# A graph-network kernel: gate stage in interleaved groups of four tiles, edge scatters moved into the node stages

## What is computed

```python
x = layernorm(x + x @ M)                  # M: product of 50,000 plane rotations, from src, dst, edge_weight
gate = sigmoid(relu(concat(x, query) @ gate_w1 + gate_b1) @ gate_w2 + gate_b2)
x0 = x * gate
h = concat(x0, query, x * query)
h = relu(rgat(h, W1, q1, k1, b1))         # relational attention: per edge score of query[dst] + key[src],
h = h + relu(rgat(h, W2, q2, k2, b2))     # softmax over the edges of a dst, weighted sum of rows of src;
h = relu(rgat(h, W3, q3, k3, b3))         # 4, 4 and 1 heads, two edge types with their own weights
x = layernorm(x + normalize(h @ proj_w + proj_b + x0))
x = layernorm(x + filtered_convolution(x, edge_attr))   # messages of src, summed by dst
x = layernorm(x + mean_of_neighbours(x))                # messages of dst, summed by src
```

## Time and profile before

| | before |
|---|---|
| three timed executions, us | 7099.04, 7114.69 (median), 7123.21 |
| the profiled execution, us | 7115.9 |
| its span in the trace, us | 7113.4 |
| TensorE busy (share of the span) | 4547.6 us (64%) |
| VectorE busy | 3329.0 us (47%) |
| ScalarE busy | 1981.2 us (28%) |
| GpSimd busy | 3666.5 us (52%) |
| granted TensorE clock, mean of the span | 0.753 of full speed |

### The profile page before, as it was taken

How to read it: one execution, slowest core, us unless ns; L and a number is a source line. 1 busy time by engine, 2 the same in 40 slices (tenths; PEclk the granted TensorE clock), 3 DMA queues, 4 the chain that set the end, 5 groups by cost and what they waited for, 6 DMA issues and landing times. The chain is left out here.

```text
span 7113.4 us, 82941 instructions
## 1 busy us (share of the span) xinstructions
PE 4547.6 (64%) x18412; PEld 3288.7 (46%) x18413; DVE 3329.0 (47%) x7794; ACT 1981.2 (28%) x4571; POOL 3666.5 (52%) x2933
## 2 busy tenths in 40 slices
PE   5699466642176677747666824448777777775553
PEld 5588444431155554435555723334455555443332
DVE  5577311126555452255554323343577777623334
ACT  0122111110055451035443112221455555510000
POOL 0344200001477664577664478870577777318885
PEclk9999767765588788978777655555799999876655
DMA  0000111111365542356553312221222222213333
GB/s 6 24 10 10 48 39 39 38 49 33 74 170 154 138 133 71 69 140 162 145 145 89 47 37 45 46 44 65 58 58 59 58 59 59 58 60 95 84 84 74
DMA packets 502900, 511.80 MB, mean 72 GB/s; under 512 B 324196, under 2 KB 387673, under 8 KB 502387
## 3 DMA queue, kind: packets, MB, share of 16 engines
q0 software_dynamic: 359872, 381.65, 22.4%
q1 hardware_dynamic: 142768, 127.70, 6.5%
HBM read 440.99 MB, written 65.22 MB: 71 GB/s over the span
## 5 line engine op out<-in xcount | busy, mean ns | idle before, releaser
L1198 POOL DMA_INDIRECT sum_gx_sb<-scratch_xw,keep_k_row_step_sb x1296 | 1617.8, 1248 | 575.2 <-issue 361.0
L1291 PE MATMUL sum_a_ps<-sum_gx_sb,sum_sel_sb 125*125 125x258 f32 (+1 forms) x4320 | 1227.9, 449 | 584.8 <-ACT sum_gx_sb L1233 229.9
L1291 PEld LDWEIGHTS sum_a_ps<-sum_gx_sb,sum_sel_sb 125*125 125x125 f32 x4320 | 947.3, 245 | 783.7 <-issue 592.6
L1233 ACT ACTIVATE sum_gx_sb<-sum_gx_sb,sum_wt_sb 125x129 f32<-125x129 f32 x3024 | 897.3, 388 | 446.5 <-DVE sum_wt_sb L1422 446.5
L2188 POOL DMA_INDIRECT filter_gx_sb<-scratch_h,keep_k_src_step_sb x432 | 523.6, 1212 | 310.7 <-DVEq L2332 164.7
L2619 POOL DMA_INDIRECT source_gx_sb<-scratch_h,source_grouped_sb x432 | 533.9, 1236 | 156.4 <-issue 122.9
L1109 POOL DMA_INDIRECT scratch_grouped<-keep_k_value_sb,keep_k_place_sb x400 | 542.2, 1356 | 132.3 <-issue 132.3
L2631 PE MATMUL source_s_ps<-source_gx_sb,source_sel_sb 125*125 125x257 f32 x864 | 375.8, 610 | 312.2 <-DMA source_gx_sb<-scratch_h,source_grouped_sb 310.6
L2237 PE MATMUL filter_ps<-filter_m_sb,filter_h_sb 128*125 128x256 f32 x1760 | 439.3, 406 | 38.6 <-DVE filter_f_sb L2301 37.4
L2631 PEld LDWEIGHTS source_s_ps<-source_gx_sb,source_sel_sb 125*125 125x125 f32 x864 | 249.8, 302 | 438.1 <-issue 173.5
L762 POOL DMA_INDIRECT order_near_i_sb<-in_dst,order_tile_i_sb x25 | 33.0, 1319 | 812.2 <-DVEq L796 804.9
(11 more groups left out here) (494 smaller groups left out, 7863.8 us busy)
## 6 DMA issues: line engine op xcount, KB each, us to landing
sum_gx_sb<-scratch_xw,keep_k_row_step_sb POOLq DMA_INDIRECT x1296, 4.3
scratch_xw<-gate_xsb_sb SPq DMA_DIRECT2D x50, 253.9 KB
scratch_xw<-attend_xsb_sb SPq DMA_DIRECT2D x50, 253.9 KB
filter_ea_sb<-in_ea_t SPq DMA_DIRECT2D x444, 24.4 KB
filter_gx_sb<-scratch_h,keep_k_src_step_sb POOLq DMA_INDIRECT x432
source_gx_sb<-scratch_h,source_grouped_sb POOLq DMA_INDIRECT x432, 4.0
sum_mk_sb<-scratch_masks SPq DMA_DIRECT2D x72, 93.9 KB
scratch_grouped<-keep_k_value_sb,keep_k_place_sb POOLq DMA_INDIRECT x400
```

What stands on the lines that cost most here:

```text
L1198: nc.gpsimd.indirect_dma_start(out=gx[:, q, j, :], out_offset=None, in_=table, in_offset=bass.IndirectOffsetOnAxis(ap=keep["row_step"][:, ...
L1233: last = nc.scalar.activation(here, here, ACT.Copy, scale=wt[q][:, h, j:j + 1])
L1291: last = mm(psa[b][0:P, half, 0:BF], sel[:, p, j, :], gx[:, q, at, half * BF:(half + 1) * BF], **flags)
```

## The change

1. The edge lists are made before the gate stage; `mt` is kept until then.
2. The gate stage is rewritten without a loop, in seven groups (six of four tiles, one of one tile). For each group the turn is made in halves of two tiles, two groups ahead; transposes, the two gate products, Relu, Sigmoid and the multiplication each work on up to 500 columns at once. The four steps of the next group's gate stand between the tables of this group's four tiles. The square root and the reciprocal become one power on GpSimd. The copy of the transposed x1 moves to ScalarE. The small products of the table are four of 16 columns in place of eight of 8. Table rows have two sets of PSUM banks and three SBUF buffers, each with its own store semaphore.
3. GpSimd issues in the gate stage six `group_edges` DMAs and one query scatter for each tile; in the first `nodes_attend` six and one (before: five), in the second four and one (before: three), in `filter_sum` none. `attention` loses its 25 scatters and the load of `qn`.
4. The queries stay in SBUF for all tiles (`qsb`) and are stored once, at the end of a node stage.

```diff
+def put_queries(nc, qe, keep, t, qsb, sem):
+    nc.gpsimd.indirect_dma_start(
+        out=qe, out_offset=bass.IndirectOffsetOnAxis(ap=keep["q_row"][:, t:t + 1], axis=0),
+        in_=qsb[:, t].rearrange("p r h -> p (r h)"), in_offset=None).then_inc(sem, 16)
 def attention(nc, mem, dr, keep, agg, heads, width, layer):
...
         def _(pool):
-            pool.wait_ge(nodes_in, 16)
-            for t in range(NT):
-                nc.gpsimd.indirect_dma_start(
-                    out=qe, out_offset=bass.IndirectOffsetOnAxis(ap=keep["q_row"][:, t:t + 1], axis=0),
-                    in_=qn[:, t], in_offset=None).then_inc(put, 16)
             for c in range(NEC):
...
-            sp.dma_start(qn[:], q_table.rearrange("(t p) s -> p t s", p=P)).then_inc(nodes_in, 16)
...
-            sp.wait_ge(put, 16 * NT)
             edges = qe[0:E, :].rearrange("(c p l) s -> c p (l s)", p=EC, l=P)
...
+GROUPS = [range(a, min(a + 4, NT)) for a in range(0, NT, 4)]
+def nodes_gate(nc, mem, dr, keep, mt):
+    LAST, GN, RING = len(GROUPS) - 1, 4, 3
...
+        def _(sp):
+            load_turned(0)
+            load_turned(1)
+            sp.dma_start(xn[:], dr["x"].rearrange("(t p) c -> p t c", p=P)).then_inc(xn_in, 16)
...
+            def store_rows(t):
+                sp.wait_ge(taken, t + 1)
+                for r in range(2):
+                    sp.dma_start(rows(dr["xw"], t, r * N), xsb[:, t % RING, r, :]).then_inc(xw_out[t % RING], 16)
...
+            for g in range(LAST + 1):
+                if g + 2 <= LAST:
+                    sp.wait_ge(y_taken, halves_of[g][-1] + 1)
+                    load_turned(g + 2)
+                sp.wait_ge(x1_made, g + 1)
+                sp.dma_start(by_node("x1", g), xn[:, tiles(g)]).then_inc(x1_out, 16)
+                sp.wait_ge(x0_made, g + 1)
+                sp.dma_start(by_node("x0", g), x0[:, 0:len(GROUPS[g])]).then_inc(x0_out, 16)
+                if g:
+                    for t in GROUPS[g - 1]:
+                        store_rows(t)
...
+        def _(pool):
+            def root(g):
+                pool.wait_ge(var_made, g + 1)
+                nc.gpsimd.tensor_tensor(rsd[:, tiles(g)], var[:, tiles(g)], power[:, 0:len(GROUPS[g])], ALU.pow).then_inc(
+                    rsd_made, 1)
+            root(0)
+            root(1)
+            for g in range(LAST + 1):
+                for j, t in enumerate(GROUPS[g]):
+                    if j == min(2, len(GROUPS[g]) - 1) and g + 2 <= LAST:
+                        root(g + 2)
+                    group_edges(nc, pool, dr, keep, range(6 * t, 6 * t + 6), grouped)
+                    pool.wait_ge(taken, t + 1)
+                    put_queries(nc, dr["qe"], keep, t, qsb, put)
...
+        def _(pe):
+            def table(t):
+                if t:
+                    pe.wait_ge(taken, t)
...
+            for g in range(LAST + 1):
+                ahead = halves_of[g + 2] if g + 2 <= LAST else []
+                own, nxt = GROUPS[g], g + 1 <= LAST
+                links = [lambda: turn_x1(g + 1), lambda: gate_hidden(g + 1), lambda: gate_outer(g + 1), lambda: turn_x0(g + 1)]
+                for j in range(GN):
+                    if j == 0 and ahead:
+                        turn(ahead[0])
+                    if nxt:
+                        links[j]()
+                    if j == 1 and len(ahead) > 1:
+                        turn(ahead[1])
+                    if j < len(own):
+                        table(own[j])
...
+        def _(dve):
+            def take(t):
+                dve.wait_ge(projected, t + 1)
+                if t >= RING:
+                    dve.wait_ge(xw_out[t % RING], 32 * (t // RING))
...
+                for j, t in enumerate(own):
+                    take(t)
+                    if j == 0 and len(ahead) > 1:
+                        residual(ahead[1])
+                    if j == min(1, len(own) - 1) and ahead:
+                        statistics(g + 2)
+                    if j == min(2, len(own) - 1):
+                        if g + 1 <= LAST:
+                            gate(g + 1)
+                        if ahead:
+                            scale(g + 2)
 def nodes_attend(nc, mem, dr, keep, agg, bias, names, width, heads, first):
...
                     pool.wait_ge(h_made, t + 1)
                     pool.dma_start(rows(dr["h1"], t), hc[:]).then_inc(kept_out, 16)
-                    group_edges(nc, pool, dr, keep, range(5 * t, 5 * t + 5), grouped)
+                    group_edges(nc, pool, dr, keep, range(6 * NT + 6 * t, 6 * NT + 6 * t + 6), grouped)
+                    if t:
+                        pool.wait_ge(table_made, 2 * t + 1)
+                        put_queries(nc, dr["qe"], keep, t - 1, qsb, put)
...
-                    group_edges(nc, pool, dr, keep, range(5 * NT + 3 * t, 5 * NT + 3 * t + 3), grouped)
+                    group_edges(nc, pool, dr, keep, range(12 * NT + 4 * t, 12 * NT + 4 * t + 4), grouped)
+                    if t:
+                        pool.wait_ge(table_made, 2 * t + 1)
+                        put_queries(nc, dr["qe1"], keep, t - 1, qsb, put)
...
 def filter_sum(nc, mem, dr, keep, agg):
...
-                if j == HF - 1 and step < 400:
-                    group_edges(nc, pool, dr, keep, range(8 * NT + step // 2 - 1, 8 * NT + step // 2 + 1), grouped)
-            pool.wait_ge(grouped, 16 * 200)
```

More of the change, by code:

```diff
@@ L1659, in _, with turn @@
         @block.tensor
         def _(pe):
+            def turn(k):
+                g, some = HALVES[k]
+                pe.wait_ge(xt_in[g % 2], 16 * (g // 2 + 1))
+                if k:
+                    pe.wait_ge(y_taken, k)
+                for j, t in enumerate(some):
+                    at = (t - GROUPS[g].start) * P
+                    for b in range(2):
+                        last = mm(psy[0:P, j, :], xt[:, g % 2, b, at:at + P], mt[:, b, :], start=(b == 0), stop=(b == 1))
+                last.then_inc(y_made, 1)
@@ L1661, in _ @@
+            turned = 0
+            for k in halves_of[0]:
+                turn(k)
             pe.wait_ge(landed, 16 * LOADS)
@@ L1741, in _, with residual, statistics @@
+            for g in range(LAST + 1):
+                take_x1(g)
+                hidden(g)
+                gate(g)
+                take_x0(g)
         @block.vector
         def _(dve):
+            def residual(k):
+                g, some = HALVES[k]
+                dve.wait_ge(y_made, k + 1)
+                here = slice(some.start, some.stop)
+                vec.tensor_tensor(xn[:, here], psy[0:P, 0:len(some), :], xn[:, here], ALU.add).then_inc(y_taken, 1)
+            def statistics(g):
+                dve.drain()
+                for t in GROUPS[g]:
+                    vec.bn_stats(stats[:, t, :], xn[:, t, :])
+                dve.drain()
+                for t in GROUPS[g]:
+                    vec.bn_aggr(mv[:, t, :], stats[:, t, :])
+                dve.drain()
+                vec.tensor_scalar(var[:, tiles(g)], mv[:, tiles(g), 1], 1e-5, None, ALU.add).then_inc(var_made, 1)
@@ L1799, in _ @@
-            residual(0)
-            with dve.Fori(0, NT - 1) as t:
-                gate(t)
-                residual(t + 1)
-                take(t)
-            gate(NT - 1)
-            take(NT - 1)
+            for k in halves_of[1]:
+                residual(k)
+            statistics(1)
+            gate(0)
+            scale(1)
+            for g in range(LAST + 1):
+                ahead = halves_of[g + 2] if g + 2 <= LAST else []
+                own = GROUPS[g]
+                if ahead:
+                    residual(ahead[0])
+                for j, t in enumerate(own):
[7 more added lines that the diff above has]
+                            gate(g + 1)
+                        if ahead:
+                            scale(g + 2)
@@ L2730, in build @@
             source_order(nc, mem, dr, keep)
+        with phase("gate") as mem:
+            nodes_gate(nc, mem, dr, keep, mt)
         agg = keeper.sb("agg", [P, NT + 1, 516])
```

298 lines of the change are left out of this document (166 added, 132 removed).

## The result

The changed kernel takes 6789.5 us (median of four runs, 6778.4 to 6793.9), the kernel before 7110.3 beside it. The ratio is 0.9548, with a 95% interval of 0.9530 to 0.9566. The forecast was 6762 with a range of 6708 to 6850: the sign and the range held, the time forecast was 27.5 us too low. The profiled execution spans 6788.7 us against 7113.4, so 324.7 us went where the sum had 353.

A forecast was written before the change was run, and what follows sets the result against it. No engine was full: the gate stage was a chain in which TensorE idles. Gate -284, edge stages -117, attends +30 and +18 sum to -353 us from 7115.9, forecast 6762 us, range 6708 to 6850.

The forecast's parts named there:

- Gate stage, TensorE's work: Gate stage: tables, turn, gate products and transposes give TensorE 43.7 us of work for four tiles.
- The wait for `turn_x0`: Gate stage, ahead of each group's fourth table: TensorE has nothing for some 3 us while VectorE finishes the third take.
- The ring: Gate stage: the fourth tile's take needs the first row's store, behind a 500 KB store; 1 us allowed.
- The tail: End of the gate stage: 6 us until the stores have landed and the next stage begins.
- GpSimd in the gate: Gate stage: GpSimd needs 44.4 us a group beside TensorE's 48.5, with 4 us of room.
- The rival that DMAs are delayed by VectorE: Gate stage and attends: delayed DMAs average 1.66 us, GpSimd becomes the bound, +47 us, 6809 in total; chance 0.20.
- Edge stages: Three edge stages: query loads or gathers start earlier, -37, -37 and -43 us, sum -117.
- Attends: Both attends: GpSimd's added DMAs set the pace, +30 us in the first and +18 in the second.
- Filter: Filter: VectorE's own instructions cover the scatters, so removing 200 DMAs gives 0 us.
- The clock rival: Gate and attends: TensorE's clock stays low, gate +75 us, attends +10, total 6845; chance 0.17, shared with exposed links.

The follow-up runs named there:

- rows_first: Changed kernel with SyncE storing a group's first three tables before it waits for x0 of the next group: 6752.1 us, gate stage 411.6.
- ring4: Changed kernel with four table buffers instead of three, order of stores unchanged: 6770.6 us, gate stage 410.8.
- no_gate_edges: Changed kernel with the gate stage's 150 edge scatters put into the filter instead: gate stage 428.2 us.
- the undo: Changed kernel with the query scatters and the load of `qn` back at the start of the edge stage: 6869.8 us.
- best: Changed kernel plus tables ahead of x0, next group's gate before the third take, queries stored by tile, edge scatters 150, 100, 50, 100: 6742.8 us, ratio 0.9472.
- best2: As best, but the second attend keeps its one store of q at the end: 6677.6 us, ratio 0.9377.

## Why the prediction held, and which steps failed

- **Gate stage, TensorE's work: right.** 43.7 us a group was forecast and 43.71 measured once only waits of 0.6 us were left in it; the terms agree one by one (16 passes of a table 6.9, a gate product 3.6), that it fits to the digit is luck. The start, 110 us to the first table against 107, too.
- **The wait for `turn_x0`: right.** "some 3 us" were 2.2 to 2.94 in each of seven groups, 19.4 us in all. Left out was what follows a stall: passes at the lower level, about 1 us a group (47.67 - 43.71 - 2.94).
- **The ring: this step failed.** "It is behind a store of 500 KB and has 7.7 us minus the copy; I allow 1 us." The landing took 13 to 15 us and TensorE's wait 4.1 to 8.7 us. I saw the place in the queue, but put no time on the 500 KB and the 508 KB of the first tile's two table stores: 1 MB in the 13.4 us from the issue of x0's store to VectorE's start is 77 GB/s. rows_first and ring4 remove it, -43 and -44 us; no_gate_edges shows that the added scatters, which I had priced for GpSimd alone, slow the landing as well. In the loop this is the larger part of +30.
- **The tail: failed.** "6 until the stores have landed" were 21.5. "SyncE issues fewer DMAs than before (... one of q ...)" was counted as a saving; the 3125 small rows take 6 to 7 us at the end, where nothing covers them (in the first attend from 2744 to 2750.5, at 12 to 29 GB/s in stretches of 1 us); ten stores of 254 KB stand ahead of them, issued late for the reason above. The same store hid in the attends: 8.9 of the first attend's +19.1 are tail, and 7.1 of the second's +17.7.
- **GpSimd in the gate: right, with less room than "4 us".** Level at 43.7, where its last scatter lags by 10 us, +47.5 us with eight scatters. The rival that DMAs are delayed by VectorE fell, since its condition is rarely met: the 175 of the stage take 1.19 us in the mean, 1.49 with the gap, not 1.66. Three beside the four scaling operations took 1.28 to 1.30 us instead of 1.18, and two that were issued while VectorE multiplied x1 by the gate 1.62 and 2.15 us (rows below this list). That rival's total, 6809, is 19.5 us off, nearer than the forecast's 27.5, and for another reason.
- **Edge stages: right**, -110.7 against -117, and the undo gives 114.5.
- **Attends: inside the bounds (+36.8 against +48), with a shift.** In the first the takes came 0.4 us a tile later, 10 us; at 1.48 us a DMA, and no gap ahead of the store, a tile of GpSimd is 11.0, not 12. The 1.58 that I took for "this stage's own price" held three gaps of 3.4 to 4.5 us on top of the 0.30 between two DMAs, and those don't multiply with their number. That error of -20 and the tail's +9 make the -11. The second came out at +17.7 against +18 by luck: 7.1 of it are tail, a term that the sum did not have, and its loop rose by 10.6 only.
- **Filter: the mechanism right, the number wrong.** The scatters hide: with 0, 50, 100 or 150 of them it takes 1168.5 to 1173.1 us, all far from 1182.8. So their removal did not bring the -13.2; the earlier trace rows showed it already, 21.13 us with and without. Each turn is 0.13 us shorter with VectorE's instructions the same and its gaps between some of them smaller. The cause stays open; no run here isolates it.
- **The clock rival** had its mechanism half right: the granted clock rose to 0.93, as forecast, and the rest of it, about 18 us, was lost behind the two stalls.
- **Slips in the sums that move nothing:** the first attend's own terms end at +33, not +35; the lower bound of the parts leaves out the -5 for the order of the stages; and the kernel before issues 150 DMAs in its loop with the loads, not 125.

The longer of the two delayed scatters, in the changed kernel:

```profile
1499.20 1.20 DVE L1884 TENSOR_TENSOR gate_x0t_sb<-gate_x1t_sb,gate_gt_sb 128x1000 f32<-128x1000 f32 x1 [0.22 <-issue]
1499.32 2.15 POOL L1116 DMA_INDIRECT scratch_qe<-gate_qsb_sb,keep_k_q_row_sb  x1 [0.47 <-DVEq L1896]
```

Both end 1.04 to 1.07 us behind VectorE's operation, and the gather of the earlier trace rows 1.1 us behind its own, as if they had waited for its end; why, is not shown.

## What to carry to other kernels

Price a ring of buffers by the landing of the store, with all that stands ahead of it in the queue and the bytes it shares the DMA engines with, not by its issue; one buffer more, or the urgent store first, was worth 43 us here. Where per-tile stores of narrow rows are gathered into one, look at where it lands: at a stage's end it is in the open. And work moved onto a queue brings its waits along: the query scatter closed a ring through the kept load, harmless until small stores doubled the time to that load's landing.

## What the runs showed of the hardware

- 3125 rows of 32 bytes in one store took 6.5 us at 12 to 29 GB/s at the end of the first attend (2744 to 2750.5); the last table stores, rows of 2080 bytes, ran at 81 to 115 GB/s just before (2738 to 2742).
- A load on GpSimd's queue landed 7.1 us (median) behind its issue where SyncE stored 125 rows of 8 bytes in each tile, and 3.7 us where it did not (best and best2, second attend).
- An indirect DMA of GpSimd costs mostly 1.17 to 1.23 us and 0.30 of gap in all node stages, 1.28 to 1.30 beside VectorE's `tensor_scalar` from SBUF to SBUF (1.54 us for four), and up to 2.15 when issued during a `tensor_tensor` of 1.20 us from SBUF to SBUF.
- TensorE ran at the lower level behind waits of 4 us (3.15 us for four passes of 512 columns instead of 1.88), and behind most waits of 2.9 us (granted clock 0.50 from 1394.7 to 1397.8; but 1.00 from 1447.3 to 1455.0, behind 2.94 us). With its waits down to 0.6 us it had 1.00 for 263 us.
